# Head and cross attention of a decoder block in one program block, weights held in the probability tiles as pairs of heads

## What is computed

```
x = x + self_attention(layernorm(x))          # one head, scores times a 64-wide band mask
x = x + cross_attention(layernorm(x), ctx)    # 16 heads of 64, ctx is 16 x 1444 x 128, key mask
x = x + experts(layernorm(x))                 # 16 experts, top 2, and a shared one
...
Q = (input_Q @ W_Q.T + b_Q); K = (input_K @ W_K.T + b_K); V = (input_V @ W_V.T + b_V)
scores = where(attn_mask, -10000, Q K^T / 8); out = softmax(scores) V; return out @ W_out.T + b_out
```

## Time and profile before

| what | value |
|---|---|
| timed runs | 1580.31, 1582.99, 1580.31 us; median 1580.31 |
| the profiled execution | 1585.67 us, its span 1583.9 us |
| PE, PEld busy | 1460.1 us (92% of the span), 1406.2 us (89%) |
| DVE, ACT, POOL busy | 1130.9 us (71%), 881.6 us (56%), 991.3 us (63%) |
| mean granted TensorE clock | 0.963 |

### The profile page before, as it was taken

How to read it: one execution, slowest core, us unless ns; L and a number is a source line. 1 busy time by engine, 2 the same in 40 slices (tenths; PEclk the granted TensorE clock), 3 DMA queues, 4 the chain that set the end, 5 groups by cost and what they waited for, 6 DMA issues and landing times. The chain is left out here.

```text
span 1583.9 us, 30091 instructions
## 1 busy us (share of the span) xinstructions
PE 1460.1 (92%) x10586; PEld 1406.2 (89%) x10586; DVE 1130.9 (71%) x2764; ACT 881.6 (56%) x1663; POOL 991.3 (63%) x1125
## 2 busy tenths in 40 slices
PE   7779999999999999999999999999999999966696
PEld 6669999999999999999999999999999999965585
DVE  1358777877787777777786868687868686759465
ACT  1145565565656565656565656565656565626353
POOL 1267575767576767676676757675757675525564
PEclk9589999999999999999999999999999999977898
DMA  3111111111111111211111111111111101024322
GB/s 81 49 36 54 40 57 36 55 48 53 38 52 48 53 34 41 60 41 52 32 61 43 55 36 55 39 52 33 51 39 53 33 32 34 10 75 130 90 62 90
DMA packets 99935, 80.46 MB, mean 51 GB/s; under 512 B 16882, under 2 KB 98603, under 8 KB 99787
## 3 DMA queue, kind: packets, MB, share of 16 engines
q1 hardware_dynamic: 97178, 74.16, 15.9%
q0 software_dynamic: 2112, 4.29, 0.8%
q10 hardware_dynamic: 496, 0.10, 0.0%
HBM read 67.37 MB, written 11.15 MB: 50 GB/s over the span
## 5 line engine op out<-in xcount | busy, mean ns | idle before, releaser
L1033 ACT CAST pT_hi<-banks 128x512 fp32r<-128x512 f32 (+1 forms) x672 | 363.2, 544 | 321.3 <-PE banks L1212 316.1
L1107 DVE TENSOR_TENSOR pT_lo<-banks,pT_hi 128x512 fp32r<-128x512 f32 (+1 forms) x576 | 359.4, 627 | 236.6 <-ACT pT_hi L1033 230.6
L964 POOL TENSOR_SCALAR probs<-probs,row_inv 128x1408 f32<-128x1408 f32 x192 | 278.8, 1452 | 235.3 <-DVE row_inv L1099 235.0
L942 POOL TENSOR_SCALAR bias<-mask,c_all 128x1444 f32<-128x1444 uint8 (+1 forms) x208 | 307.1, 1476 | 118.8 <-DVE nmax L1092 108.9
L1212 PE MATMUL banks<-ident,probs 128*128 128x128 f32 (+1 forms) x2304 | 364.8, 274 | 10.2 <-POOL probs_half L966 4.8
L1236 PE MATMUL banks<-pT_hi,ctx_hi 128*128 128x256 f32 (+1 forms) x1056 | 327.6, 310 | 2.6 <-DVE ctxT_lo L1133 2.6
L1024 ACT ACTIVATE probs<-probs,nmax 128x1448 f32<-128x1448 f32 x192 | 289.9, 1510 | 56.3 <-DVE nmax L1092 55.8
L1236 PE MATMUL banks<-pT_lo,ctx_hi 128*128 128x256 f32 (+1 forms) x1056 | 302.0, 286 | 0.0
L1236 PE MATMUL banks<-pT_hi,ctx_lo 128*128 128x256 f32 (+1 forms) x1056 | 301.8, 286 | 0.0
L1212 PEld LDWEIGHTS banks<-ident,probs 128*128 128x128 f32 (+1 forms) x2304 | 270.0, 140 | 23.5 <-DVE pT_lo L1107 12.0
L1196 PE MATMUL banks<-ctxT_hi,qh 128*128 128x362 f32 x832 | 241.1, 371 | 10.1 <-POOL ql L1001 9.9
(11 more groups left out here) (284 smaller groups left out, 2352.0 us busy)
## 6 DMA issues: line engine op xcount, KB each, us to landing
mask<-in_mask_BxSxS_bk SPq DMA_DIRECT2D x192, 180.5 KB
nat<-in_ctx SPq DMA_DIRECT2D x16, 704.0 KB
up_raw<-in_L_ffn_W SPq DMA_DIRECT2D x32, 128.0 KB, 2.2
xs_dram<-empty SPq DMA_DIRECT2D x20, 130.0 KB, 1.7
rows<-xs_dram SPq DMA_DIRECT2D x10, 260.0 KB, 2.9
down_raw<-in_L_ffn_W SPq DMA_DIRECT2D x16, 128.0 KB, 2.4
t_both<-yk_dram SPq DMA_DIRECT2D x3, 512.0 KB, 4.8
mask<-in_mask_BxSxS_bk SPq DMA_DIRECT2D x16, 90.2 KB
```

Source lines behind the costliest of these rows:

```text
L942: pool.tensor_scalar(bias[(t + i) % 2][0:n, 0:SK], masks[m % MSLOTS][0:n, :], MASKED, c_all[0:n, bb, t:t + 1], ALU.mult, ALU.add).then_inc ...
L964: pool.tensor_scalar(prob(j)[0:n, 0:FIRST], prob(j)[0:n, 0:FIRST], rinv[0:n, s:s + 1], 1.0, ALU.mult, ALU.mult)
L1033: act.copy(pT_hi[tslot(i, j)][:, 0:width], banks[:, T_BANK + j % 2, 0:width]).then_inc(turned_hi, 1)
L1107: dve.tensor_tensor(p_lo, turn, p_hi.bitcast(F32), ALU.subtract).then_inc(turned_lo, 1)
```

## The change

The two blocks become one (`attention`). What `first_unit` did is split into `first_sync`, `first_gpsimd`, `first_scalar`, `first_vector`, `first_tensor`, called at the head of each engine's part. The barrier between the blocks goes.

Weights no longer have tiles of their own: class `First` lays them into the six `probs` tiles, which hold nothing before the first score. A weight is now 128 partitions high, a pair of heads; W_Q and W_V have the other head's half of the rows zero (`wQz`, `wVz`, cleared by DVE and POOL), so a matmul over 128 rows gives one head. W_K and W_Q are loaded by five DMAs from ACT's queue, W_V by four; context 0 is now loaded by SP ahead of W_out and W_V. R_SMALL has 25 matmuls, R_WOT 8 transposes and two copies, R_CONST 9 matmuls. On PE, rounds 1 and 2 of unit 0 go ahead of the first R_A round. For batch 0 all eight query rounds have their own `qf`, so the wait on `q_split` is left out; preps use five banks; round 7 of unit 0 and its `set` stand after prep 2, and `const`, the store of x1 and the load of unit 1's x after the last prep round.

In the periods, DVE's `add` goes from place 36.9 to 36.3, `band`, `lo` and `c` 0.6 to 0.7 places earlier; `stat2`, `aggr2`, `nrm2` and `const` go from places 42.9 to 58.9 of the even period to 1.9 to 20.9 of the odd one, with POOL's reciprocal root (48.5 to 5.2); round 7 goes from place 44.3 to 36.2 of the odd period. SP stores x1 after c's turn and loads the next x at mask 9.

```diff
-UNIT_AT = (11.5, 14.5, 16.5, 23.5, 36.2, 11.5, 14.5, 44.3)
+UNIT_AT = (11.5, 14.5, 16.5, 23.5, 36.2, 11.5, 14.5, 36.2)
...
-UNIT_STAGES = ((0, 1.9, "stat1"), (0, 3.9, "aggr1"), (0, 7.9, "nrm1"), (2, 17.3, "band"), (2, 18.9, "max"),
-               (2, 22.1, "recip"), (4, 36.9, "add"), (4, 42.9, "stat2"), (4, 46.9, "aggr2"), (4, 54.3, "nrm2"),
-               (4, 58.9, "const"), (5, 12.2, "lo"), (6, 15.2, "c"), (7, 45.0, "set"))
+UNIT_STAGES = ((0, 1.9, "stat1"), (0, 3.9, "aggr1"), (0, 7.9, "nrm1"), (2, 16.6, "band"), (2, 18.9, "max"),
+               (2, 22.1, "recip"), (4, 36.3, "add"), (5, 1.9, "stat2"), (5, 3.9, "aggr2"), (5, 7.9, "nrm2"),
+               (5, 11.6, "lo"), (6, 14.6, "c"), (5, 20.9, "const"), (7, 36.3, "set"))
...
+        self.wK = part(0, 0, 8, D)
+        self.wQz = [part(1, 0, 8, D), part(2, 0, 8, D)]
+        self.wVz = [part(3, 0, 8, D), part(4, 0, 8, D)]
...
+        self.qf = [part(1 + n // 4, 2 * S * (n % 4), 2, S) for n in range(QROUNDS)]
...
+    act.dma_start(f.wK, W_K.rearrange("(p r) d -> r p d", r=128)).then_inc(f.wqk_in, 16)
+    act.wait_ge(f.q_cleared, 2)
+    for half in range(2):
+        for a in range(2):
+            act.dma_start(by_parity(f.wQz[half], a), by_head_rows(W_Q, a, half)).then_inc(f.wqk_in, 16)
...
-                        if t == 0 and turned_over is not None:
-                            store_x1(sp, w, turned_over, x1_dram)
-                        if t == 4 and turned_over is not None and turned_over + 1 < NU2:
-                            load_x(sp, w, turned_over + 1, x)
...
                             turn_c(sp, w, turned_over, c_dram)
+                            store_x1(sp, w, turned_over, x1_dram)
...
+                        if t == 9 and turned_over is not None and turned_over + 1 < NU2:
+                            load_x(sp, w, turned_over + 1, x)
...
-                                wait(dve, q_split, b + db, QROUNDS, n - 1)
+                                if b + db > 0:
+                                    wait(dve, q_split, b + db, QROUNDS, n - 1)
```

More of the change, by code:

```diff
@@ L1 @@
+import math
 from contextlib import ExitStack
@@ L250, in decoder @@
             nat = held("nat", [128, KT, D])
-            n2 = [held(f"n2{i}", [128, 2, S], F32R) for i in range(2)]
             empty = held("empty", [128, 2, RW])
-            nat_in = attentions.enter_context(nc.semaphore("nat_in"))
-            rows_in = [attentions.enter_context(nc.semaphore(f"rows_in{i}")) for i in range(2)]
-            empty_made = attentions.enter_context(nc.semaphore("empty_made"))
             w = Units(nc, attentions, ident, c_all)
[L257 to L262, removed]
+            attention(nc, x, ctx_in, mask, wq_s, wk_s, wv_s, W_Q, b_Q, W_K, b_K, W_V, b_V, W_out, b_out,
+                      banks, ident, A_hi, A_lo, VO, u, c_all, w, x1_dram, n2hi_dram, n2lo_dram, c_dram,
+                      x2_dram, xs_dram, nat, empty, xs_zeroed)
         experts(nc, Wg, W1, b1, W11, b11, W2, b2, Ws1, bs1, Ws11, bs11, Ws2, bs2,
@@ new lines, in first_bias, with first_scalar, split_hi @@
+def first_bias(pool, f):
+    pool.wait_ge(f.w_done, f.R_BIAS + 1)
+    for n, t in enumerate(f.bVrep):
+        pool.tensor_copy(t, f.bcol[:, 2, 4 * n:4 * n + 4].unsqueeze(2).to_broadcast([128, 4, S])).then_inc(f.bias_made, 1)
+def first_scalar(act, f, w, W_Q, W_K, A_hi, VO):
+    def split_hi(r, dst, scale=1.0):
+        act.wait_ge(f.w_ready, r + 1)
+        act.activation(dst, f.bank(r, a=4), ACT.Copy, scale=scale).then_inc(f.w_hi, 1)
+    act.dma_start(f.wK, W_K.rearrange("(p r) d -> r p d", r=128)).then_inc(f.wqk_in, 16)
+    act.wait_ge(f.q_cleared, 2)
+    for half in range(2):
+        for a in range(2):
+            act.dma_start(by_parity(f.wQz[half], a), by_head_rows(W_Q, a, half)).then_inc(f.wqk_in, 16)
+    unit_scalar(act, w, 0, 0, f.unit(0))
+    unit_scalar(act, w, 0, 1, f.unit(1))
+    unit_scalar(act, w, 0, 2, f.unit(2))
+    split_hi(f.R_A, A_hi[:, 0:4, :], 0.125)
+    unit_scalar(act, w, 0, 3, f.unit(3))
+    for n in range(1, 4):
+        split_hi(f.R_A + n, A_hi[:, 4 * n:4 * n + 4, :], 0.125)
+    unit_scalar(act, w, 0, 5, f.unit(5))
+    for n in range(4):
+        split_hi(f.R_VO + n, VO[:, 4 * n:4 * n + 4, 0, :])
@@ L755, in cross_attention, with attention @@
+def attention(nc, x, ctx_in, mask, wq_s, wk_s, wv_s, W_Q, b_Q, W_K, b_K, W_V, b_V, W_out, b_out,
+              banks, ident, A_hi, A_lo, VO, u, c_all, w, x1_dram, n2hi_dram, n2lo_dram, c_dram,
+              x2_dram, xs_dram, nat, empty, xs_zeroed):
     with ExitStack() as ctx:
@@ L1053, in emit @@
                                 dst = qh[i][:, 0:S * H].rearrange("p (q h) -> p h q", h=H)[:, 2 * n:2 * n + 2, :]
-                                act.copy(dst, qf[n % 2][:, :, :]).then_inc(prep_hi, 1)
+                                act.copy(dst, qf_of(b + db, n)).then_inc(prep_hi, 1)
+                first_scalar(act, f, w, W_Q, W_K, A_hi, VO)
                 periods(act, emit)
@@ L1146, in emit @@
                                 wait(dve, qf_begun, b + db, QROUNDS, n + 1)
-                                dve.tensor_tensor(qf[n % 2][:, :, :], parts[:, 1, :, :], qf[n % 2][:, :, :],
+                                dve.tensor_tensor(q, parts[:, 1, :, :], q,
                                                   ALU.add).then_inc(prep_read, 1)
+                            if b == -1 and j == 2:
+                                unit_vector(dve, w, 0, "set", f.unit(7))
+                            if b == -1 and j == PREP - 1:
+                                dve.wait_ge(f.w_done, f.R_CONST + 1)
+                                unit_vector(dve, w, 0, "const", None)
                         elif kind == "project":
```

443 lines of the change are left out of this document (227 added, 216 removed).

## The result

The changed kernel took 1539.51 us in the median of four runs (1536.11 to 1540.59), the one before 1580.49 (1580.31 to 1582.99, four runs). The ratio is 0.973, with a 95% interval from 0.9711 to 0.9748. The forecast was 1545, with a range from 1531 to 1563. The profiled execution took 1540.29 us, its span 1538.1, against 1585.67 and 1583.9 before.

A forecast was written before the change was run, and what follows sets the result against it. PE was taken to set the pace in the batches and a chain of waiting PE rounds to make the opening; 21 us there plus 14 in the batches, 35 less, took the median from 1580.31 to 1545, range 1531 to 1563.

The forecast's parts named there:

- The opening: Start to first score: pieces sum to 50.2 us, first score at 63.6 and not 84.58, 21.0 less; bounds 14.4 to 23.5.
- the batches: Moved pieces in the periods: 2.0 us less per two periods, seven times, 14 less; bounds 4 to 24.7.
- The start: Ahead of the first score: R_A's start kept at 13.4 us, although when W_Q and W_K land was unknown.
- the forecast's early end: Opening: weights all there when unit round 2 is done, some 2.5 us before 13.44, a gain of 23.5.
- The step that failed: Opening: PE runs at the lower clock level (1.2 GHz) however busy, so the pieces keep their prices.
- the clock rises: Rival, opening: a longer unbroken run halves 46 us of PE pieces, 23 more won, 1522 us; chance 0.04.
- Query rounds and tail: Opening, batch 0: query rounds 7.05 us at PE's pace, 0.88 a round, and 3.8 from DVE's last round to first score.
- `add`: Batches, DVE: going ahead of one `pT_lo`, it ends 0.6 us earlier and PE's prep 1 wait shrinks by 0.6 a pair.
- Round 7: Batches, odd period: at its new place its wait of 0.73 goes, `set` adds 0.17, net gain 0.56 us a pair.
- The query rounds and what odd periods get: Batches: `qf` waits go, 1.46 us gained a pair; `nrm2` in odd periods loses 0.66, `const` counted as nothing.
- The opening alone: Rival: moved pieces make as much waiting in odd periods as they took from even ones; 1559 us, chance 0.15.
- The slower one: Rival, odd periods: SP waits for `const` before issuing mask 7, so masks and POOL's biases come late; 1594 us, chance 0.03.

The follow-up runs named there:

- The execution with a wait of 0.81 for W_Q: Changed kernel plus 40 transposes of the identity on PE in its wait ahead of the first score; 1540.08 us, ratio 0.9723.
- the changed kernel with 64 rows: Changed kernel with matmuls of R_A, R_SMALL's second 16 and R_VO over rows 0 to 63 alone; first score 62.38, one run, 1549.96 us.
- the kernel before with 128: Kernel before with weight and bias tiles 128 rows high, rows 64 to 127 zero; first score 74.29, one run, 1573.84 us.
- batches only: Kernel before with only the change's places of unit pieces in the periods, POOL's reciprocal root and SP's order; 1571.65 us, ratio 0.9919.
- nrm at 5.6: Changed kernel with nrm1 and nrm2 whole at place 5.6 and not 7.9, nothing else; 1528.73 us, ratio 0.9665.

## Why the prediction was right, and where it failed

The time fell in the forecast's range, 5.5 us below its value. In the profiled executions the gain was 45.4 (45.8 of the span) where the sum had 35. The opening had 11.6 more than forecast, the batches 1.0 less. The opening's 32.6 lies outside the 14.4 to 23.5 that the prediction had allowed it. The sum stayed in the range because the range's end also held 24.7 for the batches, which gave 13.0. That is luck, and not a sign that the opening was understood.

**The start.** R_A at 13.4 was right, but not for the reason given. The forecast tied it to the landing of the weights; in the changed kernel PE does not wait for them (row at 13.38), so they were there when unit round 2 was done. That is the condition of the forecast's early end, 2.5 us sooner. It came no sooner because PE's first matmul, which waits for the self attention's W_V, began at 6.86 us and not at 4.17. The two errors cancel, by luck. The execution with a wait of 0.81 for W_Q shows that the weights have little to spare. The first matmul before, then after:

```profile
4.17 0.45 PE L701 MATMUL banks<-ident,wsq 128*128 128x128 f32 x1 [4.17 <-DMA wsv<-in_L_attn_WV]
...
6.86 0.66 PE L731 MATMUL banks<-ident,probs 128*128 128x128 f32 x2 [6.86 <-DMA wsv<-in_L_attn_WV]
```

**The pieces of the opening**, as summed up in the prediction and as measured:

| piece | forecast | after |
|---|---|---|
| R_A with rounds 3 and 4 | 10.4 | 5.7 |
| R_SMALL | 10.7 | 6.9 |
| unit rounds 5 and 6 | 2.1 | 2.8 |
| R_WOT | 2.6 | 2.8 |
| R_VO | 7.0 | 6.0 |
| R_CONST, round 7 | 4.1 | 2.4 |
| context preps | 2.4 | 1.5 |
| query rounds and tail | 10.9 | 10.6 |

Unit rounds 5 and 6 grew because they now run at the lower level: their first two passes take 0.57 at 25.98, and took 0.39 at 44.90.

**The step that failed** is the one on the clock: "So PE runs at the lower level through the opening, however busy." The ten busy us at 0.50 that it rested on were 64-row passes, and the change makes them 128 rows high. I had looked at the height and allowed for it as a cost, "at most 5%". The runs showed it as a gain: 10.4 us by the changed kernel with 64 rows, 10.3 by the kernel before with 128 (10.1 and 9.4 if counted from R_A's start). The rise that the rival "the clock rises" had, with a chance of 0.04, is what happened, but not by the longer unbroken run: with 64 rows PE is as busy from 13 to 33 us and stays slow. Its 23 us were too many, since R_SMALL, R_WOT and R_VO are still slow in whole or in part, and the query rounds are not PE's any more. The rule of the Trainium skill that I weighed ("TensorE: Matmul & The Clock Gate", Part 1) spoke for a rise. The trace of before spoke both ways, and I read one. Behind the 3.62 us of 128-row transposes at 39.99 the two passes at 44.90 took 0.39, the faster pace, so "through the opening" was wrong even there. But the preps from 65.22 to 74.71, also 128 rows high, stayed slow with PE busy, as these windows of before show (length, PE busy, granted clock, DMA share, GB/s):

```profile
66.00:68.00 2.00, 2.00 (x12) 0.50 0.36 98
...
72.00:74.00 2.00, 2.00 (x12) 0.50 0.00 0
```

So height moved the level in both kernels in which it was changed, and is not all that decides it.

**Query rounds and tail** came out right by two errors that cancel, which is luck: PE is through in 4.4 us (0.55 a round) where I had 7.05 (0.88), and DVE, ACT and POOL, at 0.66 to 0.71 a round, would have kept up with the second but not with the first. The bias ahead of the last `ql` was in the forecast's 3.8.

**The batches.** `add`: forecast 0.6 a pair, measured 0.7, right. Round 7: forecast 0.56, measured 1.0, right in kind; its waits were priced by PE's list. The query rounds and what odd periods get: forecast 1.46 - 0.66 = 0.8 won, measured 0.35 lost; the `qf` waits did go and the `pT_lo` waits did come (9.6 - 4.7 = 4.9 by PE's list, 0.7 a pair), as said, but PE's list hides much of the second, and `const`, counted as nothing, costs 2.2 us in all by the same list. Together 0.7 + 1.0 - 0.35 = 1.35 of the pair's 1.43, so next to nothing is left for the small moves of `band`, `lo` and `c`, which were not tried apart.

**The rivals.** The opening alone would not have given 1559 but 1547.4, with the higher clock in it. The slower one needs POOL to wait for masks; POOL's waits of the changed kernel have none from 75 to 1340 us.

**What stays open.** Why the level did not rise behind these 64-row passes, why it stayed down over the 128-row preps of before, and why it falls in R_SMALL was not tried further, and the reading of 1.00 ahead of the first fall can't be told from a true 1.00 by itself. The median gain (41.0) is below that of the profiled executions (45.4); the profiled one of before was 5.2 above its median. Of that 2.2 seem to lie in the batches (1318.1 against 1315.9 in the kernel before with 128 rows) and 0.9 in the landing of W_K (R_A at 13.44 against 12.50 in batches only); the rest was not found.

## What to carry to other kernels

Price a matmul by the length of rows like it at both levels of the clock, and when a change alters how much of the array a pass uses, treat the level as an unknown with two ends, not as a condition of the stage. Read waits from the weight loader's list as well as from PE's before a stall is traded for another; here the two had opposite signs. And before an instruction of VectorE is moved, look at what GpSimd does beside the new place: here a pair of periods won 1.9 us by that, and 1.43 by all the moves of the change.

## What the runs showed of the hardware

In R_A, passes over 64 rows stayed at 0.24 to 0.26 us each, and the mostly 64-row passes behind them at 0.21 to 0.24, through 30 us in which PE hardly paused, with the granted clock reading 1.00; R_A's passes of the same columns over 128 rows, half of them zeros, came to 0.12 to 0.135 by the third round. Once fast, 64-row passes took 0.117. Height was not all: 128-row preps ran for 9.5 us at 0.50 with PE busy, and the clock fell from 1.00 to 0.50 within R_SMALL's one-column passes over 128 rows, also with PE busy.

A VectorE instruction of 100x128 took 0.33 to 0.43 us by itself or beside POOL's bias, and 1.31 beside POOL's division. The Trainium skill ("SBUF — State Buffer", SBUF: two separate sides) has GpSimd and VectorE, the latter in a two-port mode or with two inputs in SBUF, take a shared pair of ports as a lock, the loser blocked to the end of the other's instruction. The division beside `nrm` agrees, if `nrm` runs in such a mode, which no run shows by itself. The bias does not: in the kernel with nrm at 5.6 it ran from 294.36 to 295.83, and `nrm` began at 295.48 and took 0.68 for two all the same. The profile's spans on POOL are rough, so this is one reading and no proof.
